# Layer 3's attention stage: the division moved from VectorE to ScalarE and GpSimd, and each finished tile normalised there instead of in a stage of its own

## What is computed

```python
x = x + tanh(g_ffn[2])   * _L2_ffn_ref(_layernorm(x), ...)        # 8 experts, 2 for each row
x = x + tanh(g_xattn[3]) * _L3_xattn_ref(_layernorm(x), ctx, ctx, Wq, Wk)
x = x + tanh(g_ffn[3])   * _L3_ffn_ref(_layernorm(x), ln1_weight, ln1_bias, ...)

def _L3_xattn_ref(query, key, value, Wq, Wk):     # 16 heads of 8
    scores = jnp.einsum('bhqa,bhka->bhqk', q, k) * SCALE
    cutoff = jax.lax.top_k(scores, 32)[0][..., -1:]
    masked = jnp.where(scores >= cutoff, scores, -jnp.inf)
    w = jax.nn.softmax(masked, axis=-1)
    e = jnp.einsum('bhqk,bhka->bhqa', w, v)

def _L3_ffn_ref(hidden_states, ln1_weight, ln1_bias, ...):
    ln1 = _layer_norm(hidden_states, ln1_weight, ln1_bias)
```

## Time and profile before

| | |
|---|---|
| median of 3 runs | 3078.91 us (3070.96 to 3082.48) |
| the profiled execution | 3081.14 us, its span 3079.3 us |
| busy over the span: PE, PEld | 2774.2 us (90%), 2136.3 us (69%) |
| DVE | 2031.7 us (66%) |
| ACT | 1840.5 us (60%) |
| POOL | 1428.6 us (46%) |
| mean granted TensorE clock | 0.935 |

### The profile page before, as it was taken

The page is one execution under the profiler, slowest core; times in us unless marked ns, Lnnn a source line. Parts: engine busy times, 40 slices in busy tenths (PEclk is TensorE's granted clock), DMA queues, the critical chain, the costliest instruction groups (busy, mean ns, idle before and its releaser), DMA issues. The chain is left out here.

```text
span 3079.3 us, 70583 instructions
## 1 busy us (share of the span) xinstructions
PE 2774.2 (90%) x21912; PEld 2136.3 (69%) x21912; DVE 2031.7 (66%) x7995; ACT 1840.5 (60%) x5346; POOL 1428.6 (46%) x1748
## 2 busy tenths in 40 slices
PE   7999969986998989999999999988899984597999
PEld 5888854433766668888888777666677762386776
DVE  5445536664653456666666459999999999686433
ACT  5777734443543346666666468888888874453333
POOL 2122117762442434444444238787878786452000
PEclk9999979997998999999999899999999995697999
DMA  3000024323763311111111000000000000001000
GB/s 115 6 5 6 5 52 88 82 60 113 263 220 126 120 56 55 54 54 54 54 54 54 23 10 14 14 13 13 13 13 13 13 14 33 3 18 36 8 10 10
DMA packets 99461, 151.83 MB, mean 49 GB/s; under 512 B 11312, under 2 KB 39488, under 8 KB 98752
## 3 DMA queue, kind: packets, MB, share of 16 engines
q1 hardware_dynamic: 99296, 149.96, 16.5%
HBM read 103.33 MB, written 46.47 MB: 49 GB/s over the span
## 5 line engine op out<-in xcount | busy, mean ns | idle before, releaser
L1899 POOL TENSOR_TENSOR l2a_probs<-l2a_probs,l2a_inv 128x1024 f32<-128x1024 f32 x128 | 242.3, 1893 | 369.4 <-DVE l2a_inv L2065 369.2
L2010 ACT ACTIVATE l2a_probs<-l2a_s_ps,l2a_nm 128x256 f32<-128x256 f32 x512 | 236.6, 473 | 199.2 <-DVE l2a_nm L2041 199.2
L2847 DVE MAX8 l3a_top<-l3a_work 128x8 f32<-128x128 f32 x1536 | 314.2, 276 | 0.0
L2424 POOL TENSOR_SCALAR l3a_above<-l3a_score,l3a_top 128x128 f32<-128x128 f32 x504 | 294.1, 601 | 16.6 <-DVE l3a_top L2847 8.5
L2565 PE MATMUL l3a_l2o_ps<-net_arena 128*128 128x128 f32 x1952 | 256.1, 295 | 33.8 <-ACT net_l1f_gate L2681 33.4
L2565 PEld LDWEIGHTS l3a_l2o_ps<-net_arena 128*128 128x128 f32 x1952 | 249.6, 210 | 45.5 <-ACT net_l1f_gate L2681 37.0
L2849 DVE MATCH_REPLACE8 l3a_work<-l3a_top,l3a_work 128x128 f32<-128x128 f32 x1024 | 268.9, 275 | 0.0
L2552 PE MATMUL l3a_l2h_ps<-net_cols,net_arena 128*128 (+1 forms) x1024 | 251.9, 388 | 14.7 <-ACT net_arena L2716 12.8
L2552 PEld LDWEIGHTS l3a_l2h_ps<-net_cols,net_arena 128*128 128x128 f32 x1024 | 184.8, 191 | 67.2 <-ACT net_arena L2716 25.3
L721 ACT ACTIVATE l0a_probs<-l0a_score_ps,l0a_nm 128x128 f32<-128x128 f32 x512 | 180.1, 383 | 73.5 <-DVE l0a_nm L770 73.5
L2716 ACT ACTIVATE net_arena<-l3a_l2h_ps,net_l2f_b 128x256 f32<-128x256 f32 x496 | 203.6, 492 | 12.4 <-PE l3a_l2h_ps L2552 11.0
(11 more groups left out here) (532 smaller groups left out, 7152.6 us busy)
## 6 DMA issues: line engine op xcount, KB each, us to landing
kv_ahead<-l1a_kept SPq DMA_DIRECT2D x128, 256.0 KB, 2.7
l0f_code<-code_rows SPq DMA_DIRECT2D x32, 512.0 KB, 11.2
l2a_kT<-kv_ahead SPq DMA_DIRECT2D x64, 256.0 KB, 2.6
l2a_v<-kv_ahead SPq DMA_DIRECT2D x64, 256.0 KB, 2.6
l1a_shift<-neg_top SPq DMA_DIRECT2D x16, 512.0 KB, 4.9
l1f_chosen<-mask_code SPq DMA_DIRECT2D x64, 128.0 KB, 3.1
keys_ahead<-l1f_keys_kept SPq DMA_DIRECT2D x32, 256.0 KB, 3.2
l3a_kT<-keys_ahead SPq DMA_DIRECT2D x32, 256.0 KB, 2.7
```

What stands on the lines that cost most here:

```text
L1899: pool.tensor_tensor(p[:, :, :], p[:, :, :], per_row(inv[c % 2][a][:, :, :].rearrange("p i o -> p (i o)"), KV), ALU.mult).then_inc(scaled, 1)
L2010: act.activation(probs[c % 2][a][:, 2 * i + odd, :], s_ps[a][odd][:, i * KV:(i + 1) * KV], ACT.Exp, bias=nm[c % 2][a][:, i, odd:odd + 1], ...
L2424: ins = pool.tensor_scalar(above[:, i, :], score[c % 4][:, h, :], top[c % 2][:, ROUNDS - 1, h, 7:8], None, ALU.is_ge)
L2847: ins = dve.max(t[:, step // 2, h, :], src)
```

## The change

The division is taken from VectorE. ScalarE copies the turned output with its sums out of PSUM (`take_out`, into `o_raw`); GpSimd raises the sums to the power -1 (`inv`), multiplies, and adds to `k.x` as before. Then the tile is finished within the stage: ScalarE sums its rows (`sum_rows`), GpSimd makes the negated mean (`centre`), ScalarE sums the squares of the centred rows (`square_rows`), GpSimd makes both inverse deviations with one power over two columns and writes the rows normalised once to `k.rows` and twice to `x_normed` (`normalise_last`), TensorE turns the latter (`turn_last`), and ScalarE copies it to `k.cols` with gain and shift (`take_last`). The call of `normalise` behind the stage is dropped. `FIRST` goes from 4 to 8 and `LAST_LAG` from 3 to 5, so that more passes are written out.

```diff
-    LAST_LAG = 3
+    LAST_LAG = 5
-    FIRST = BODY
+    FIRST = 2 * BODY
...
                 def add_attention(q, c):
                     wait(pool, o_ready, q, 1, c + 1)
+                    pool.tensor_tensor(inv[:, :], o_raw[:, :, DA:DA + 1].rearrange("p h o -> p (h o)"), neg_one[:, :], ALU.pow
+                                       ).then_inc(inv_ready, 1)
+                    wait(pool, inv_ready, q, 1, c + 1)
+                    wait(pool, x_done, q, 1, c)
+                    pool.tensor_tensor(o_norm[:, :, :], o_raw[:, :, 0:DA], per_row(inv[:, :], DA), ALU.mult
+                                       ).then_inc(o_read, 1)
+                    wait(pool, o_read, q, 1, c + 1)
                     xt = k.x[:, ds(tile(q, c), 1), :].rearrange("p o d -> p (o d)")
                     pool.tensor_tensor(xt, xt, o_norm[:, :, :].rearrange("p h d -> p (h d)"), ALU.add
                                        ).then_inc(x_done, 1)
+                def centre(q, c):
+                    wait(pool, x_summed, q, 1, c + 1)
+                    wait(pool, x_squared, q, 1, c)
+                    wait(pool, x_rows, q, 2, 2 * c)
+                    pool.tensor_scalar(x_mean[:, :], x_sum[:, :], -1.0 / D, None, ALU.mult).then_inc(x_centred, 1)
+                def normalise_last(q, c):
+                    wait(pool, x_squared, q, 1, c + 1)
+                    pool.tensor_scalar(x_veps[:, 0:1], x_spread[:, :], 1.0 / D, LN_EPS, ALU.mult, ALU.add).then_inc(x_veps_made, 1)
+                    pool.tensor_scalar(x_veps[:, 1:2], x_spread[:, :], (1.0 + LN_EPS) / D, LN_EPS * LN_EPS, ALU.mult, ALU.add
+                                       ).then_inc(x_veps_made, 1)
+                    wait(pool, x_veps_made, q, 2, 2 * (c + 1))
+                    pool.tensor_tensor(x_rstd[:, :], x_veps[:, :], k.neg_half[:, 0:2], ALU.pow).then_inc(x_scaled, 1)
+                    wait(pool, x_scaled, q, 1, c + 1)
+                    wait(pool, x_turned, q, 1, c - 1)
+                    t = tile(q, c)
+                    pool.tensor_scalar(x_normed[c % 2][:, :], k.x[:, t, :], x_mean[:, 0:1], x_rstd[:, 1:2], ALU.add, ALU.mult
+                                       ).then_inc(x_rows, 1)
+                    pool.tensor_scalar(k.rows[:, t, :], k.x[:, t, :], x_mean[:, 0:1], x_rstd[:, 0:1], ALU.add, ALU.mult
+                                       ).then_inc(x_rows, 1)
...
-                                (take_v, -1), (for_part(mask, 0), 1), (for_part(mask, 1), 1),
+                                (take_v, -1), (for_part(mask, 0), 1), (centre, 4), (for_part(mask, 1), 1),
                                 (add_experts, 1 - AHEAD), (in_group(add_base, 1), -AHEAD),
-                                (in_group(stage_weights, 0), -AHEAD), (add_attention, 3)], loops=0,
-                         draining=[(add_attention, 3), (for_part(negate_max, 0), 1), (for_part(mask, 0), 1)])
+                                (in_group(stage_weights, 0), -AHEAD), (normalise_last, 4), (add_attention, 3)], loops=0,
+                         draining=[(add_attention, 3), (for_part(negate_max, 0), 1), (for_part(mask, 0), 1), (finish_late, 4),
+                                   (finish, 3)])
...
+                def turn_last(q, c):
+                    wait(pe, x_rows, q, 2, 2 * c + 1)
+                    wait(pe, p_ready, q, NQ, NQ * (c + 4), most=NQ * NB)
+                    wait(pe, x_cols, q, 1, c)
+                    pe.transpose(p_ps[:, 0:P], x_normed[c % 2][:, :], k.ident[:, :]).then_inc(x_turned, 1)
...
-                              (for_part(apply, 3), 2), (for_part(scores, 2), -1), (turn_out, 2)], first=0)
+                              (for_part(apply, 3), 2), (for_part(scores, 2), -1), (turn_out, 2), (turn_last, 5)], first=0)
...
+                def take_out(q, c):
+                    wait(act, o_turned, q, 1, c + 1)
+                    wait(act, o_read, q, 1, c)
+                    act.activation(o_raw[:, :, :], o_ps[:, :, 0:DA + 1], ACT.Copy).then_inc(o_ready, 1)
+                def sum_rows(q, c):
+                    wait(act, x_done, q, 1, c + 1)
...
+                    act.activation(passed[:, :], k.x[:, ds(tile(q, c), 1), :].rearrange("p o d -> p (o d)"), ACT.Copy,
+                                   accum_out=x_sum[:, :]).then_inc(x_summed, 1)
+                def square_rows(q, c):
+                    wait(act, x_centred, q, 1, c + 1)
...
+                    act.activation(passed[:, :], k.x[:, ds(tile(q, c), 1), :].rearrange("p o d -> p (o d)"), ACT.Square,
+                                   bias=x_mean[:, 0:1], accum_out=x_spread[:, :]).then_inc(x_squared, 1)
+                def take_last(q, c):
+                    wait(act, x_turned, q, 1, c + 1)
...
+                    act.activation(k.cols[:, ds(tile(q, c) * P, P)], p_ps[:, 0:P], ACT.Identity, scale=gain, bias=shift_by
+                                   ).then_inc(x_cols, 1)
...
-                def divide(q, c):
-                    wait(dve, o_turned, q, 1, c + 1)
-                    wait(dve, x_done, q, 1, c)
-                    dve.reciprocal(inv[:, :], o_ps[:, :, DA:DA + 1].rearrange("p h o -> p (h o)")).then_inc(inv_ready, 1)
-                    wait(dve, inv_ready, q, 1, c + 1)
-                    dve.tensor_tensor(o_norm[:, :, :], o_ps[:, :, 0:DA], per_row(inv[:, :], DA), ALU.mult
-                                      ).then_inc(o_ready, 1)
-                schedule(dve, [(divide, 3), (for_part(cutoffs, 0), 0), (for_part(cutoffs, 1), 0),
+                schedule(dve, [(for_part(cutoffs, 0), 0), (for_part(cutoffs, 1), 0),
                                (in_group(measure, 1), 1 - AHEAD)], loops=0,
-                         draining=[(divide_last, 3), (negate_last, 1), (mask_last, 2)])
+                         draining=[(negate_last, 1), (mask_last, 1)])
...
-        normalise(nc, k, "n3f", gains=k.l3b_w, twice=True, gain=norms[:, 0:1], shift=norms[:, 1:2])
```

More of the change, by code:

```diff
@@ L2270, in l3_attention @@
         pT = [s.sb(f"pT{i}", [P, Q4, P]) for i in two]
-        inv = s.sb("inv", [P, H])
+        inv, neg_one = s.sb("inv", [P, H]), s.sb("neg_one", [P, H])
+        o_raw = s.sb("o_raw", [P, H, DA + 1])
         o_norm = s.sb("o_norm", [P, H, DA])
+        x_sum, x_mean, x_spread = (s.sb(n, [P, 1]) for n in ("x_sum", "x_mean", "x_spread"))
+        x_veps, x_rstd = s.sb("x_veps", [P, 2]), s.sb("x_rstd", [P, 2])
+        passed, x_normed = s.sb("passed", [P, D]), [s.sb(f"x_normed{i}", [P, D]) for i in two]
+        gain, shift_by = k.l3b_w.norms[:, 0:1], k.l3b_w.norms[:, 1:2]
+        x_summed, x_centred, x_squared, x_veps_made, x_scaled, x_rows, x_turned, x_cols = (s.sem(n) for n in (
+            "x_summed", "x_centred", "x_squared", "x_veps_made", "x_scaled", "x_rows", "x_turned", "x_cols"))
         hidden = [k.arena2[:, i * CHUNKS * WIDE:(i + 1) * CHUNKS * WIDE].rearrange("p (c n) -> p c n", c=CHUNKS)
@@ L2320, in l3_attention, with wait @@
         BASE_STEPS, NORM_STEPS = 3, 10
-        def wait(eng, sem, q, per_element, value):
+        def wait(eng, sem, q, per_element, value, most=None):
             n = q * int(BODY * per_element) + value
+            if isinstance(q, int) and most is not None:
+                n = min(n, most)
             if not isinstance(q, int) or n >= 1:
@@ L2524, in turn_probs @@
                 def turn_probs(q, c, n):
+                    if n == 0:
+                        wait(pe, x_cols, q, 1, c - 3)
                     wait(pe, masked, q, NQ, NQ * c + n + 1)
@@ L2655, in _ @@
                 wf.wait(act)
+                k.l3b_w.wait(act)
                 act.wait_ge(shifted, 1)
@@ L2767, in _ @@
                 take_bias(0, 1)
-                schedule(act, [(for_part(exps, 0), 1), (for_part(exps, 1), 1), (for_part(take_y, 0), 1 - AHEAD),
+                schedule(act, [(take_out, 3), (for_part(exps, 0), 1), (for_part(exps, 1), 1), (sum_rows, 4), (for_part(take_y, 0), 1 - AHEAD),
                                (for_part(exps, 2), 1), (for_part(exps, 3), 1),
@@ L2776, in _ @@
                                (for_part(gelu, 7), -AHEAD), (in_group(take_bias, 1), -AHEAD),
[L2777 to L2780 removed]
+                               (for_part(take_p, 3), 2), (in_group(take_weights, 0), -AHEAD), (take_o, 2), (square_rows, 4), (for_part(take_scores, 2), -1), (take_last, 5)], first=0,
+                         draining=[(take_out, 3), (for_part(take_p, 0), 2), (for_part(exps, 0), 1), (for_part(exps, 1), 1),
+                                   (late(sum_rows), 4), (for_part(take_p, 1), 2), (late(square_rows), 4), (for_part(take_p, 2), 2),
+                                   (for_part(take_p, 3), 2), (sum_rows, 3), (take_o, 2), (square_rows, 3),
+                                   (for_part(exps, 2), 1), (for_part(exps, 3), 1), (take_last, 5)])
             @block.vector
```

31 lines of the change are left out of this document (18 added, 13 removed).

## The result

The changed kernel takes 3191.9 us (median of 4 runs, 3179.1 to 3194.5) against 3078.8 for the one before: ratio 1.0361, 95% interval 1.0335 to 1.0387, so 113 us or 3.6% slower. The prediction was 3188, range 3138 to 3226. The profiled execution has a span of 3192.8 us, against 3079.3 before.

The account below looks back on a forecast made before the run. The prediction took VectorE as the bound before the change and GpSimd after it. Terms of +115.7, +3.5 and -10.2 us sum to +109, giving 3188 us in the median's terms, range 3138 to 3226.

Parts of the forecast that it names:

- room of 3.0 us: GpSimd's idle time per tile in stage l3a before the change, read from its waits for VectorE's maxima: 3.0 us.
- a: Sum of GpSimd's new work per tile (division, mean, normalising): 6.1 us, with 5.8 as low and 7.3 as high price.
- Odd steps: Odd passes of the l3a schedule, where GpSimd also has norm_scale and add_base: 31.2 us after the change, no wait for squares.
- The even step: Even passes of the l3a schedule: 28.9 us, with GpSimd waiting 2.8 us for ScalarE's squares; 26.1 without that wait.
- the squares land at 22.6: In even steps of l3a, ScalarE's squares are ready 22.6 us into the step, while GpSimd is there at 19.8.
- rival of its own: Ring slower still: TensorE's lowered clock delays ScalarE, 1.6 us in each of 25 steps, +40; 3220 and more; chance 14%.
- Term 1: Steps 4 to 28 of l3a, 13 even and 12 odd: 750.1 us in place of 634.4, +115.7.
- Term 2: Step 3 of l3a, which gets only a division: +3.5 us.
- Term 3: From step 29's start to the next stage, norm stage dropped: 112.5 us in place of 122.7, -10.2.
- the drain: The end of l3a after step 31, from division 29 through the last tile's chain to the next stage: 41.6 us.
- the estimate of 18.3 us for the last exponentials: In the drain, the last exponentials stand on ScalarE behind square_rows of tile 29, until about 18.3 us.
- ScalarE's and TensorE's new work costs nothing: In l3a these engines' waits for GpSimd cover their new operations; without that cover, 1.6 us a tile on ScalarE.

## Why the prediction was right

**GpSimd becomes the bound, from a cost per tile above its room of 3.0 us.** Shown: the inversion taken off it gives 91 us, the squares early 51, and both together 126, which brings the stage back to VectorE's cadence. The division by itself, 3.47 us from 2244.86 to 2248.33, lies 0.5 above the room and costs 13 us; normalising by itself, 2.24 from 2242.62 to 2244.86 and 0.24 for the mean, lies below and costs nothing once the squares are early. Of the two rules of the Trainium skill that the prediction weighed, "GPSIMD Engine Reference", Engine selection, which gives elementwise work to VectorE, was the one that held for the power. Its factor of about two for two inputs is not what these runs show: the power took 2.91 us on GpSimd where the reciprocal took 0.24 on VectorE, the multiplication 0.41 against 0.29. The other rule of the Trainium skill, "Perfetto Trace Analysis", Optimizing Scalar/DVE Operations, that offloading a full VectorE even to GpSimd may make sense (the section adds that it might not help between these two), holds in these runs as far as the room goes: 0.37% faster with normalising alone, 3.6% slower with the division on top and the squares late.

**The prices.** The power 128x16 was 2910 ns where the norm stage had 2914. The two normalising operations with two operands by row were mis-sized: 451 and 450 ns where I took 600 from the nearest rows. The squares took 0.48 us for 0.45; their price was said to be that of 8 ACTIVATEs, but the row, L379 in the earlier trace rows, has 20 at 483 ns. So a is 5.9 and not 6.1 (2.2 for normalising, 3.5 for the division, 0.2 for the mean). Odd steps are 30.8 where 31.2 was forecast: 0.2 of the difference are a's, and the rest lies ahead of x_veps, which GpSimd reaches 24.5 us into the step and not 24.8.

**The even step.** The wait was found where it was said to be, released by what was said, but it was mis-sized: 28.9 forecast, 29.8 measured. The step "the squares land at 22.6" held where TensorE came out of its idle time best (22.4) and missed its clock in the others, up to 24.3. The prediction had the clock as a rival of its own, 1.6 us in each of 25 steps; the run with 44 transposes shows 0.8 and 2.0 us in turn in the even steps 6, 10, ... 26, 1.4 in the mean, and 0.1 in odd ones, where ScalarE has time. Part of it was in the forecast unseen: the 22.6 were read off a step whose own burst took 5.32 us. The changed kernel's steps with bursts of 5.4 us are 28.7 long, near the 28.9; those with 6.1 to 6.7 are the ones that were missed. Step 28 had no wait at all, 26.0 in place of 28.9: ScalarE has no Gelu left in it, and its squares are done 18.2 us into the step. Term 1 came to +118.4 (115.7 forecast): two errors of opposite sign, 5 us less in the odd steps and 8 us more in the even ones.

**Term 2** is the length of step 3 from its second negation, 28.4 for 24.8: +3.6, forecast +3.5. **Term 3:** steps 29 to 31 took 70.0 (70.9) and the drain 41.7 (41.6), together 111.7 for 122.7: -11.0 in place of -10.2. The chain on the last tile, from the power at 2772.68, is 8.7 us. That these are so near owes something to luck: the estimate of 18.3 us for the last exponentials was no reading of rows. They began 17.2 us into the drain, and from there to the last division's power it took 15.8 us where the forecast has 15.0: two errors of opposite sign again.

**ScalarE's and TensorE's new work costs nothing.** Borne out, as far as VectorE's cadence goes: with all of it present, and only the inversion back on VectorE and the squares early, VectorE is busy for 100 us of 100. Where ScalarE's squares stood in its order did cost, as forecast.

What stays open: whether it is the fetch of instructions for which TensorE stands 3.5 us at the loop's start in the run with 44 transposes. The 0.6 us, too, by which ScalarE's table load comes before or behind its wait was seen, not tried.

## What to carry to other kernels

Before work is moved off a full engine, take the idle time of the engine that gets it, per tile, from its waits, and set the sum of the prices of the new work against it: below that room the move was free here, above it every microsecond counted in every tile, so that two halves which cost 13 and 7 us cost 113 together. Where the new work needs a result of a third engine, put that engine's part as early in its order as its inputs allow: one entry moved in a list was worth 51 us in the changed kernel, and 16 where GpSimd had only the normalising. And one costly instruction can be sent back alone: the power took 2.9 us for 16 elements a partition, where VectorE's reciprocal and multiplication together took 0.48.

## What the runs showed of the hardware

A TENSOR_SCALAR on GpSimd with two operands by row over 128x128 took 0.45 us, less than those with one such operand, 0.60 and 0.62 in the earlier trace rows; these differ in more than that, the first is a comparison and the second leaves gaps between the heads in what it writes. ScalarE's sum along a row is an instruction of its own in the trace, ACTIVATION_READ_ACCUMULATOR, 0.19 us behind each ACTIVATE of 0.29 (sum) or 0.39 (squares). The granted clock rose again only as the burst behind the idle time ended, 0.92 in the third piece above, so that what stood first behind the idle time paid for it. And 44 transposes for nothing, 5.0 us of TensorE in a step, shortened nine of the twelve even steps: work added to an engine that waits is not always lost. The same 44 brought 33 packets of instructions into a stretch of the loop that had none with 24, and TensorE stood 3.2 to 3.5 us at each of four returns of the loop.
